# The FFN's second bias: from a product in the output bank to an addition on GpSimd, in a transformer block on one core

## What is computed

```python
x = x + 0.5 * ffn(layernorm(x))      # block "a"
x = x + attention(layernorm(x))      # block "att", 16 heads of 64, causal, gated distance bias
x = x + 0.5 * ffn(layernorm(x))      # block "c", the same weights

def ffn(x):                          # H = 512, D = 128; m1, m2 are products of 16 early tokens of x
    h = gelu(x @ W1.T + scale * x @ m1.T + b1)
    return h @ W2.T + scale * h @ m2.T + b2
```

## Time and profile before

| | |
|---|---|
| time, median of 3 runs | 797.78 us (797.62 to 799.66) |
| the profiled execution | 796.84 us, of which the span from the first to the last instruction is 794.8 us |
| granted clock of TensorE, mean | 0.994 of full |
| PE, DVE, ACT, POOL busy | 765.8, 667.6, 655.8, 641.5 us |
| matmuls | 9669 |
| bias products | 16 |

### The profile page before, as it was taken

One profiled execution on the slowest core, in us unless ns is written; L12 is line 12 of the kernel. 1 busy time (PEld: TensorE's weight loads), 2 busy tenths in 40 slices (PEclk: granted clock), 3 DMA queues, 4 the chain that ended last, 5 costly groups with the idle time before them and its releaser, 6 DMA issues.

```text
span 794.8 us, 25588 instructions
## 1 busy us (share of the span) xinstructions
PE 765.8 (96%) x9669; PEld 549.4 (69%) x9669; DVE 667.6 (84%) x1874; ACT 655.8 (83%) x1420; POOL 641.5 (81%) x751
## 2 busy tenths in 40 slices
PE   4789999999999999999999999999999999999997
PEld 2346767677767776677677777677776776777775
DVE  8779788987988887988989878888888889899965
ACT  6759877888998889897998889988897989986762
POOL 5528868978988979789888889889797897887791
PEclk9899999999999999999999999999999999999999
DMA  7071616464173633637153541736336371548420
GB/s 191 13 162 42 134 44 141 62 135 97 29 161 69 149 68 73 144 78 154 29 132 72 126 105 28 162 68 148 70 68 149 69 162 29 122 83 151 87 48 27
DMA packets 97297, 77.12 MB, mean 97 GB/s; under 512 B 71662, under 2 KB 84080, under 8 KB 97176
## 3 DMA queue, kind: packets, MB, share of 16 engines
q1 hardware_dynamic: 96696, 73.92, 43.6%
q10 hardware_dynamic: 480, 1.57, 0.8%
HBM read 4.74 MB, written 2.10 MB: 9 GB/s over the span
## 4 chain that ended last, share of the span: by engine, by line
PE 84%; ACT 4%; issue 3%; DVE 3%; DMA 2%; POOL 2%; SPq 1%; POOLq 0%; ACTq 0%; DVEq 0%
PE ps L1048 15%; PE ps L1049 14%; PE ps L1050 14%; PE ps L1197 8%; PE ps L1170 8%; PE ps L1198 8%; PE ps L1152 6%; PE ps L1199 3%; PE ps L1172 2%; DMA qk<-qkn 2%; PE ps L1065 1%; PE ps L1179 1%; ACT qkn L934 1%; PE ps L1075 1%; ACT sq L933 1%
## 5 line engine op out<-in xcount | busy, mean ns | idle before, releaser
L813 POOL TENSOR_TENSOR pt_l<-pt 128x512 f16<-128x512 f32 x368 | 320.3, 900 | 70.0 <-ACT pt L1008 69.8
L1008 ACT ACTIVATE pt<-ps 128x512 f32<-128x512 f32 (+1 forms) x384 | 175.1, 530 | 29.3 <-PE ps L1199 17.1
L839 POOL TENSOR_TENSOR qkn<-qkn,rs 128x512 f32<-128x512 f32 x128 | 130.5, 1048 | 30.9 <-ACT rs L945 30.9
L1197 PE MATMUL ps<-qk 128*128 128x512 f16 (+3 forms) x512 | 146.9, 300 | 0.0
L1198 PE MATMUL ps<-qk 128*128 128x512 f16 (+3 forms) x512 | 146.5, 299 | 0.0
L1508 DVE CUSTOM_DVE_ANT_0 masked<-ps,causal_row 128x512 f16<-128x512 f32 x224 | 130.4, 619 | 18.0 <-PE ps L1170 15.7
L1048 PE MATMUL ps<-v_buf,pt 128*128 128x65 f16 x1280 | 129.8, 194 | 0.9 <-POOL pt_l L813 0.8
L1049 PE MATMUL ps<-v_buf,pt 128*128 128x65 f16 x1280 | 129.8, 193 | 0.0
L1050 PE MATMUL ps<-v_buf,pt_l 128*128 128x65 f16 x1280 | 129.5, 193 | 0.0
L1048 PEld LDWEIGHTS ps<-v_buf,pt 128*128 128x128 bf16 x1280 | 118.0, 98 | 6.6 <-issue 1.2
L1049 PEld LDWEIGHTS ps<-v_buf,pt 128*128 128x128 bf16 x1280 | 117.5, 98 | 3.2
(11 more groups left out here) (198 smaller groups left out, 2053.6 us busy)
## 6 DMA issues: line engine op xcount, KB each, us to landing
qk<-qkn SPq DMA_DIRECT2D x186, 256.0 KB, 4.1
x_in<-in_L_attn_x SPq DMA_DIRECT2D x8, 256.0 KB, 3.0
out<-x_out SPq DMA_DIRECT2D x8, 256.0 KB, 2.4
qk<-qkn ACTq DMA_DIRECT2D x6, 256.0 KB, 4.9
qk<-qk SPq DMA_DIRECT2D x1, 1024.0 KB, 8.5
qk<-gtt SPq DMA_DIRECT2D x64, 8.0 KB
qk<-nmt SPq DMA_DIRECT2D x64, 2.0 KB
y_hl<-ytt SPq DMA_TRANSPOSE x63, 3.1
```

The lines of the kernel that those rows point to most:

```text
L813: g.tensor_tensor(pt_l[:, h % 2, c], pt[:, h % 2, c], pt_h[:, h % 2, c], ALU.subtract).then_inc(s_pt_l, 1)
L839: g.tensor_tensor(qk, qk, r.unsqueeze(4).broadcast_to([P, 2, 2, 2, D]), ALU.mult).then_inc(s_qkn, 1)
L1008: a.activation(pt[:, h % 2, c], ps[:, j, 0:width], ACT.Exp).then_inc(s_exp, 1)
L1197: pe.matmul(dst, k1(h)[:, keys], q1(h)[:, kb * P:T], start=True, stop=False)
```

## The change

The bias no longer goes through PE. `half_b2` holds b2 on all 128 partitions (one DMA that spreads the row), DVE halves it once ("b2"), and POOL adds it in place to the residual, once per batch and block, as the new stage "xb", after the normalisation has read that tile. DVE's addition of the FFN output waits for it (`s_biased`). In the 14 units that aren't shared the 48 products run token block by token block (t outside, r inside), the first of each token block opens its own sum, and PE waits for all four low parts before the first. The two shared units keep the old order and open the bank with a product of zeros: the first 128 columns of `causal_row` are all zero. The tiles `b2ld`, `b2cut`, `b2rows`, `ones` and their memsets go. All engines get new orders in lead, first and body; final changes on POOL alone.

```diff
+        s_biased = {n: sem(f"s_biased_{n}") for n in ("a", "c")}
...
-            for at in (0, LO_ROW):
-                sp.dma_start(b2ld[at:at + 1, :], row_of(b2)).then_inc(s_wffn, 16)
+            sp.dma_start(half_b2[:, :], row_of(b2).broadcast_to([P, C])).then_inc(s_wffn, 16)
...
+            def add_bias(part, s, b, n):
+                if b == 0 and n == "a":
+                    pool.wait_ge(s_b2, 1)
+                pool.wait_ge(s_z[n], (b + 1) * TB)
+                src = x_in if n == "a" else attended(b)
+                g.tensor_tensor(src[:, :, :], src[:, :, :], half_b2[:, :].unsqueeze(1).broadcast_to([P, TB, C]), ALU.add).then_inc(s_biased[n], 1)
...
-                if b == 0 and n == "a":
-                    pe.wait_ge(s_b2, 1)
                 part.room(pe, s)
-                pe.matmul(part.bank(s), ones[:, :], b2rows[:, :, :].rearrange("p t c -> p (t c)"), start=True, stop=False)
-                for r in range(FB):
-                    if shared(n, b):
+                if shared(n, b):
+                    pe.matmul(part.bank(s), causal_row[:, 0:P], causal_row[:, :], start=True, stop=False)
+                    for r in range(FB):
                         pe.wait_ge(s_hid_l_dve, r + 1 + (0 if n == "a" else FB))
-                    else:
-                        pe.wait_ge(s_hid_l[n], (shifts(n, b) - 1) * FB + r + 1)
...
+                else:
+                    pe.wait_ge(s_hid_l[n], shifts(n, b) * FB)
                     for t in range(TB):
                         c = slice(t * P, (t + 1) * P)
-                        mm = product(part.bank(s)[:, c], hid_h[:, r, c], hid_l[:, r, c], w2_h[:, w], w_l[:, 1, w], False,
-                                     r == FB - 1 and t == TB - 1)
+                        for r in range(FB):
+                            w = slice(r * P, (r + 1) * P)
+                            mm = product(part.bank(s)[:, c], hid_h[:, r, c], hid_l[:, r, c], w2_h[:, w], w_l[:, 1, w], r == 0, r == FB - 1)
...
+            def half_bias(part, s, b):
+                dve.wait_ge(s_wffn, 16 * 6)
+                d.tensor_scalar(half_b2[:, :], half_b2[:, :], 0.5, None, ALU.mult).then_inc(s_b2, 1)
...
+                dve.wait_ge(s_biased[n], b + 1)
                 part.full(dve, out)
```

```diff
-            ("zt", "a", NEXT), ("setup", NEXT), ("m", "a", NEXT), ("warm", 0, 6, NEXT), ("h", "a", NEXT),
+            ("warm", 1, 8, NEXT), ("zt", "a", NEXT), ("setup", NEXT), ("m", "a", NEXT), ("h", "a", NEXT),
+            ("warm", 0, 6, NEXT), ("out", "a", NEXT), ("uu", NEXT), ("zt", "att", NEXT), ("qk", 0, 0, NEXT),
```

and the eight "warm" behind ("qk", 1, 3) go. DVE's "b2" moves behind "h" in the lead; ACT's "wo" (the projection weights) moves from behind "ln1" of "att" to right behind "h". POOL's lead, and its body list as far as it concerns "xb":

```diff
-            ("ul", NEXT), ("clear", NEXT), ("m", "a", NEXT), ("ud", NEXT), ("wvl", NEXT), ("wol", NEXT),
+            ("m", "a", NEXT), ("ul", NEXT), ("xb", "a", NEXT), ("ud", NEXT), ("wol", NEXT), ("clear", NEXT),
...
-            ("m", "a", NEXT), ("yt", 1, THIS), ("pl", 4, THIS), ("h", "a", NEXT), ("pl", 5, THIS), ("pl", 6, THIS),
-            ("pl", 7, THIS), ("pl", 8, THIS), ("yt", 2, THIS), ("pl", 9, THIS), ("yt", 3, THIS), ("qkn", 0, 0, NEXT),
+            ("yt", 0, THIS), ("yt", 1, THIS), ("pl", 4, THIS), ("h", "a", NEXT), ("xb", "a", NEXT), ("pl", 5, THIS),
+            ("pl", 6, THIS), ("pl", 7, THIS), ("yt", 2, THIS), ("pl", 8, THIS), ("xb", "c", LAST), ("yt", 3, THIS),
...
-            ("pl", 12, THIS), ("pl", 13, THIS), ("yt", 5, THIS), ("m", "c", LAST), ("pl", 14, THIS),
-            ("pl", 15, THIS), ("yt", 6, THIS), ("h", "c", LAST), ("m", "c", THIS),
+            ("pl", 12, THIS), ("pl", 13, THIS), ("yt", 5, THIS), ("m", "c", LAST), ("xb", "c", LAST),
+            ("pl", 14, THIS), ("pl", 15, THIS), ("yt", 6, THIS), ("h", "c", LAST), ("m", "c", THIS),
+            ("xb", "c", THIS),
```

More of the change, by code:

```diff
@@ L108 @@
-            ("qkn", 3, 1, NEXT), ("t", 4, NEXT), ("nm", 1, NEXT), ("gate", 1, NEXT), ("t", 5, NEXT),
-            ("v", 1, 0, NEXT), ("t", 6, NEXT),
+            ("ln1", "a", NEXT), ("setup", NEXT), ("sel", NEXT), ("wq", 0, NEXT), ("zt", "a", NEXT),
+            ("gp", "a", NEXT), ("m", "a", NEXT), ("h", "a", NEXT), ("wo", NEXT), ("wq", 1, NEXT), ("wq", 2, NEXT),
+            ("ln1", "att", NEXT), ("zt", "att", NEXT), ("qk", 0, 0, NEXT), ("qk", 0, 1, NEXT), ("qk", 0, 2, NEXT),
+            ("qk", 0, 3, NEXT), ("qkn", 0, 0, NEXT), ("qk", 1, 0, NEXT), ("qkn", 0, 1, NEXT), ("qk", 1, 1, NEXT),
@@ new lines @@
+            ("qk", 1, 2, NEXT), ("qk", 1, 3, NEXT), ("qkn", 1, 0, NEXT), ("qkn", 1, 1, NEXT), ("t", 0, NEXT),
+            ("t", 1, NEXT), ("gate", 0, NEXT), ("v", 0, 0, NEXT), ("rows", 0, NEXT), ("v", 0, 1, NEXT),
+            ("t", 2, NEXT), ("t", 3, NEXT), ("rows", 1, NEXT), ("qk", 2, 0, NEXT), ("qk", 2, 1, NEXT),
+            ("qk", 2, 2, NEXT), ("qk", 2, 3, NEXT), ("qkn", 2, 0, NEXT), ("nm", 0, NEXT), ("v", 0, 2, NEXT),
+            ("qk", 3, 0, NEXT), ("qkn", 2, 1, NEXT), ("qk", 3, 1, NEXT), ("qk", 3, 2, NEXT), ("s", 0, NEXT),
@@ L144 @@
+            ("gate", 1, NEXT), ("nm", 1, NEXT), ("t", 5, NEXT), ("t", 6, NEXT),
         ],
@@ L237 @@
+            ("yt", 2, THIS), ("pl", 8, THIS), ("qkn", 0, 0, NEXT), ("pl", 9, THIS), ("yt", 3, THIS),
+            ("qkn", 0, 1, NEXT), ("qkn", 1, 0, NEXT), ("qkn", 1, 1, NEXT), ("gate", 0, NEXT), ("pl", 10, THIS),
+            ("yt", 4, THIS), ("pl", 11, THIS), ("pl", 12, THIS), ("yt", 5, THIS), ("qkn", 2, 0, NEXT),
+            ("pl", 13, THIS), ("pl", 14, THIS), ("qkn", 2, 1, NEXT), ("qkn", 3, 0, NEXT), ("pl", 15, THIS),
+            ("qkn", 3, 1, NEXT), ("yt", 6, THIS), ("gate", 1, NEXT),
         ],
@@ L246 @@
+            ("pl", 9, THIS), ("qkn", 0, 0, NEXT), ("qkn", 0, 1, NEXT), ("pl", 10, THIS), ("qkn", 1, 0, NEXT),
+            ("qkn", 1, 1, NEXT), ("gate", 0, NEXT), ("m", "c", LAST), ("pl", 11, THIS), ("pl", 12, THIS),
+            ("h", "c", LAST), ("yt", 4, THIS), ("pl", 13, THIS), ("pl", 14, THIS), ("qkn", 2, 0, NEXT),
+            ("qkn", 2, 1, NEXT), ("yt", 5, THIS), ("qkn", 3, 0, NEXT), ("yt", 6, THIS), ("qkn", 3, 1, NEXT),
+            ("pl", 15, THIS), ("gate", 1, NEXT),
         ],
@@ L308, in macaron @@
     RPT = P // FB
-    LO_ROW = 32
     FIRST = 1
@@ L350, in macaron @@
         b1c = sb("b1c", [P, FB])
[L351 to L354 removed]
+        half_b2 = sb("half_b2", [P, C])
         sc = sb("sc", [P, 1])
```

289 lines of the change are left out of this document (130 added, 159 removed).

## The result

| | before | after |
|---|---|---|
| time, median of 10 runs each, same chip | 798.50 us (797.62 to 800.08) | 803.36 us (800.77 to 804.94) |
| ratio | | 1.0060, 95% interval 1.0047 to 1.0074 |
| span of the profiled execution | 794.8 us | 802.9 us |
| granted clock, mean | 0.994 | 0.979 |
| PE, POOL busy | 765.8, 641.5 us | 767.5, 662.0 us |

A forecast was written before the change was run, and what follows sets the result against it. PE, busy 96% of the span, was taken as the bound. The terms -5.4 - 0.2 + 0 + 1.04 - 1.0 = -5.6 us took the 797.8 us median to 792.2 us, 0.7% less; range 789 to 798.5.

The forecast's parts named there:

- Step 1: 14 of 16 bias products leave PE: 13 x 0.415 = 5.4 us less, the fourteenth, in the tail, counted 0.
- Step 2: Two outer units keep a first product of zeros on 128 rows: 0.2 us less each, the last counted as -0.2.
- Step 3: Second FFN product token block by token block, PE waiting for all four low parts: 0, with 0.26 us of cover.
- Step 4: POOL's 16 additions at 1.04 us each: 0 in the body, +1.04 us in the tail (bounds 0 and 1.75).
- Step 5: Lead: DVE's bias rows go behind and shrink, ACT's weight copy moves earlier: -1.0 us, bounds -2.3 and +1.3.
- Step 6: New orders in first and body on all engines: 0, since PE's elements and number of small-shape changes stay the same.
- A: Rival: POOL becomes the bound, PE stalls 1.5 us in each of 7 batches, +10.3, so 802.5 us; chance 0.12.
- C: Rival, clock: two slow lead stretches vanish, 790.2 us (more gain, chance 0.13), or one more appears, +1.7, 793.9 us.
- B: Rival: no change within 0.3%, new stalls of 3.5 us from the orders and nothing gained in the lead, 796.7 us; chance 0.15.

The follow-up runs named there:

- e10: e6 with GpSimd's additions of the half bias left out, so the output lacks what they bring; 793.69 us, ratio 0.9933.
- e5: The kernel before with its bias product kept but over 128 rows in place of 33, same orders; 793.85 us, ratio 0.9945.
- e1: After with every engine's lead list of before, and "xb" of "a" behind "ud" on GpSimd; 797.76 us, ratio 0.9995.
- e3: After with "sel" ahead of "setup" again in ACT's lead, nothing else moved; 801.77 us, ratio 1.0045.
- e15: After with before's lead, "b2" directly behind "setup", "xb" directly behind "clear", and the tail's addition late; 794.28 us, ratio 0.9950.
- e7: Before's code, bias product kept and no POOL addition, in after's first and body orders; 801.9 us, ratio 1.0041.
- e9: After with GpSimd's additions left out, all orders kept, so the output lacks what they bring; 798.53 us, ratio 0.9993.
- e8: After with before's lead orders, clearing and addition behind "ud" on GpSimd, and the tail's addition late; 797.91 us, ratio 0.9987.
- e6: After's code with before's first and body orders, otherwise the lead and tail of e8; 799.07 us, ratio 1.0004.
- e11: e8 with fourteen more products into a spent bank where TensorE was idle in the lead; 797.36 us, ratio 0.9986.

## Why the prediction was wrong

**Step 1, 13 x 0.415 = 5.4 us, right in its price.** 0.40 us a product in e10, the 0.2 us of pauses by themselves in e5. PE's busy time in the middle fell by these 5.4 us too. But after's middle is only 2.2 us shorter. The way there: e10 shows 3.1 us (input 0's part of the middle is 1.15 us longer in place of 0.4 shorter, by the wait of step 3, and the last batch 0.5 longer), and additions and new orders take another 1.0. Steps 4 and 6 had both at nothing there.

**Step 2** gave 0.2: from the start of DVE's last addition into x_in to the end of the span it is 16.98 us before, 16.78 after.

**Step 3, the wait at 0, wrong in one place.** The 0.26 us of cover was read in a body batch, and holds there. Input 1's unit, whose list is another one, had none: 0.99 us. I had looked at no unit of that list.

**Step 4, the addition, too small and the wrong neighbours.** 16 additions take 1.27 us, not 1.04 (line 794; columns as in the earlier trace rows):

```profile
L794 POOL TENSOR_TENSOR x_in<-x_in,half_b x9: 1266/1271/1287, 20.8 to 793.6; 128x512 f32<-128x512 f32 x9
L794 POOL TENSOR_TENSOR x<-x,half_b x7: 1262/1267/1707, 207.7 to 771.9; 128x512 f32<-128x512 f32 x7
```

16 x 1.27 = 20.3 us, the 20.5 us of busy time. My nearest row had one f32 tile and one broadcast statistic per head as inputs. In the body 0 was nearly right in the new orders (0.06 us a batch) and not in the old ones (0.56), whose idle I had reckoned with. In the tail +1.04 was right: with after's list and the full clock (e1 to e3) it is 1.0 us longer than before's. The profiled +3.8 has 2.8 us of half clock on top, which the longer wait doesn't explain.

**Step 5, the lead at -1.0 with bounds -2.3 and +1.3, is the step that failed.** It measured +6.4 in the profile, and e1, which undoes it, gains 5.2 us by the medians. I followed DVE's bias rows and ACT's copy on the chain and didn't price the other moves of the same lists: the clearing, named in the diff, was taken past four stages of POOL's queue onto DVE's z_att steps (3.0 us); "sel" went behind "setup" on ACT, and TensorE's "m" waits for it (e3: first h product at 13.12 in place of 14.16); the addition waits for "b2" behind DVE's hidden low parts. And the clock: 0.66 between 10 and 20 us, where before had full clock. That the moved steps brought the lower clock isn't shown; time at half clock fell with them in e1's runs, from 26.3 to 12.1 us. The gain itself was there to be had: e15's lead is 1.6 us shorter than before's.

**Step 6, orders at 0, wrong too.** In the four batches it is nearly right: +0.2 us with the bias product (e7 less its late start) and +0.5 without it and without additions (e9 against e10). Over the whole middle the profiles have +3.6 us (e7 against before) and +1.2 (e9 against e10). Late starts behind a DMA whose cover fell from 3.8 to 0.6 us are 2.4 of the 3.6 and, in e9, 1.3. I had counted PE's elements and looked at SP's store, and not at how far ahead of its user each DMA is issued. What the orders bring is room for the additions: -1.5 us in the four batches (e8 against e6).

**The rivals.** A's 802.5, 4.7 us above before, is close to the measured +4.9 by luck. It puts +10.3 into the batches, where after gained; a GpSimd without idle is what e6 shows, not after. C named the clock and bounded it by one more stretch, +1.7; the runs have 12.9 us more at half clock, in lead and tail. B's mechanism, new stalls of 3.5 us in the middle, is nearest to what after has there, 3.3 us more idle on PE, though not spread evenly; its time of 796.7 still misses the lead. The range was too narrow above, because the lead's bounds came from the steps on the chain alone.

## What to carry to other kernels

Price every stage that a list moves, not only those on the present chain: for each, which instructions of other engines it will lie beside, above all a long GpSimd step beside DVE's tensor_scalar. For a DMA whose issue moves, compare how far ahead of its user it stands with its slowest landing. A wait widened from "one by one" to "all" needs its cover read in every kind of unit, the first ones too. Where PE idles in the lead or the tail, allow a few us for the clock either way, and take several runs before explaining less than that. Where a small-shaped product sits between large ones, first try it at full shape: e5 changed two sizes, beat the change as it was made and equals it as mended in e15.

## What the runs showed that I had not expected

- Four 128x128 tensor_scalar steps of DVE: 1.1 us alone (before), 4.5 us beside GpSimd's memsets (after), which read nothing.
- The DMAs that turn the attention's output land after 3.1 us at the median in before, the slowest of 63 after 6.9; two that took 4.6 and 4.8 us in e7 met a cover of 0.6 us and held PE up for 1.1 and 1.3.
- A GpSimd addition of a 128x512 f32 tile and a broadcast row: 1.27 us, a fifth more than its scaling by one number per head (1.04).
- Ten runs of after differ by 4.2 us in span, with a granted clock of 0.979 to 0.987 that goes with it; fourteen idle products returned the clock (12.7 to 5.4 us at half clock, e8 to e11) without a gain in the median.
